# Transformer tower on one core: the second MLP product in token order, and its normalisation by statistics instructions

## What is computed

```python
x = x + attn
h2 = _ln(x, g2, beta2)                              # "norm 2"
x = x + (gelu(h2 @ w1 + b1) @ w2 + b2)              # D=256, FF=1024
...
h = h + x                                           # h: the residual of the whole tower
z = _layernorm(h)                                   # "norm 3", without gain and shift
logits = z @ gate_w.T                               # 8 experts + 1 shared
out = routed_experts(z, logits) + shared_expert(z)  # shared: silu(z @ sg) * (z @ su) @ sd
h = h + out
```

## Time and profile before

| what | value |
|---|---|
| median of 3 runs | 2754.92 us (2751.39 to 2756.34) |
| the profiled execution, its own time | 2745.01 us, of which 2743.3 us are its span |
| PE busy | 2396.6 us, 87% of the span |
| DVE busy | 1957.5 us, 71% |
| POOL busy | 1574.0 us, 57% |
| ACT busy | 1462.2 us, 53% |
| mean granted TensorE clock | 0.955 |

### The profile page before, as it was taken

One profiled execution on the slowest core, in us unless ns is written; L12 is line 12 of the kernel. 1 busy time (PEld: TensorE's weight loads), 2 busy tenths in 40 slices (PEclk: granted clock), 3 DMA queues, 4 the chain that ended last, 5 costly groups with the idle time before them and its releaser, 6 DMA issues. The chain is left out here.

```text
span 2743.3 us, 61193 instructions
## 1 busy us (share of the span) xinstructions
PE 2396.6 (87%) x22832; PEld 1736.1 (63%) x22832; DVE 1957.5 (71%) x4174; ACT 1462.2 (53%) x2731; POOL 1574.0 (57%) x1548
## 2 busy tenths in 40 slices
PE   3799999999999999999999858898988998985664
PEld 3588888878888888888887724444444444443453
DVE  2578778777877787778778735777777777775443
ACT  3566666666666666666666534443444444432232
POOL 1465656565665656565656422566556656656566
PEclk8999999999999999999999968999999999998887
DMA  4121122111221111111110020121112111100676
GB/s 146 43 67 58 40 64 61 61 43 58 62 63 40 44 37 47 36 45 39 40 44 13 10 98 24 48 85 54 48 48 84 53 43 47 38 9 16 128 136 100
DMA packets 115060, 152.21 MB, mean 55 GB/s; under 512 B 16537, under 2 KB 75917, under 8 KB 114768
## 3 DMA queue, kind: packets, MB, share of 16 engines
q1 hardware_dynamic: 88880, 124.46, 14.3%
q0 software_dynamic: 23808, 21.74, 4.4%
q10 hardware_dynamic: 2080, 2.10, 0.2%
HBM read 81.71 MB, written 90.96 MB: 63 GB/s over the span
## 5 line engine op out<-in xcount | busy, mean ns | idle before, releaser
L958 POOL TENSOR_TENSOR qkl<-fz,qkh 128x512 f16<-128x512 f32 x256 | 307.6, 1202 | 299.4 <-DVE qkh L857 299.4
L1812 POOL DMA_INDIRECT slot_dram<-xt,slot_u x256 | 257.9, 1007 | 75.8 <-issue 75.5
L529 PE MATMUL pF<-nh,qk_h 128*128 128x256 f16 x1024 | 281.2, 275 | 5.7 <-DVE nl L844 4.4
L531 PE MATMUL pF<-nl,qk_h 128*128 128x256 f16 x1024 | 280.6, 274 | 0.0
L530 PE MATMUL pF<-nh,qk_l 128*128 128x256 f16 x1024 | 280.5, 274 | 0.0
L970 POOL TENSOR_TENSOR ol<-on,oh 128x256 f16<-128x256 f32 x256 | 181.9, 711 | 147.2 <-ACT oh L794 147.1
L977 POOL TENSOR_TENSOR kvl<-kvacc,kvh 128x260 f16<-128x260 f32 x192 | 147.0, 765 | 122.3 <-ACT kvh L802 120.7
L771 ACT ACTIVATE sh<-sm 128x512 f16<-128x512 f32 x256 | 159.4, 623 | 83.6 <-DVE sm L880 83.6
L854 DVE SCALAR_TENSOR_TENSOR fz<-pF,ez 128x512 f32<-128x512 f32 x256 | 175.2, 684 | 34.1 <-ACT ez L754 32.6
L1792 POOL TENSOR_TENSOR al<-az,ah 128x512 f16<-128x512 f32 x64 | 79.2, 1238 | 206.8 <-DVE ah L1585 206.8
L529 PE MATMUL pS<-qkh 64*128 64x128 f16 x1024 | 187.7, 220 | 0.9 <-DVE sm L880 0.9
(11 more groups left out here) (315 smaller groups left out, 8667.9 us busy)
## 6 DMA issues: line engine op xcount, KB each, us to landing
xs<-in_x SPq DMA_DIRECT2D x128, 256.0 KB, 2.7
slot_dram<-blank SPq DMA_DIRECT2D x8, 1360.0 KB, 6.9
xg<-slot_dram SPq DMA_DIRECT2D x40, 272.0 KB, 3.4
h_dram<-hT SPq DMA_DIRECT2D x32, 256.0 KB, 2.3
x_dram<-x SPq DMA_DIRECT2D x32, 256.0 KB, 2.2
at_dram<-at SPq DMA_DIRECT2D x32, 256.0 KB, 2.1
x0b<-x_dram SPq DMA_DIRECT2D x16, 512.0 KB, 4.0
atb<-at_dram SPq DMA_DIRECT2D x16, 512.0 KB
```

The lines of the kernel that those rows point to most:

```text
L529: pe.matmul(out, wh, mh, start=first, stop=False, skip_group_check=True)
L531: return pe.matmul(out, wh, ml, start=False, stop=last, skip_group_check=True)
L958: nc.gpsimd.tensor_tensor(qkl[:, pair:pair + 2, cols], fz[:, n % 2, :, :], qkh[:, pair:pair + 2, cols], ALU.subtract).then_inc(fl_ready, 1)
L1812: nc.gpsimd.indirect_dma_start(io["slot_dram"], bass.IndirectOffsetOnAxis(slot_u[:, c, k:k + 1], 0), xt[:, i % 2, c, :], None, bounds_chec ...
```

## The change

The second MLP product is made with the tokens on the partitions: `gh`, `gl` are now the stationary operand and `w2_h`, `w2_l` the moving one, in 96 matmuls of 256 columns where there were 48 of 512. The residual sum `hx` comes into the same banks first, by eight float32 matmuls with a scaled identity. ACT copies the banks to `ht` (two buffers), DVE takes mean and variance of each token by `bn_stats` and `bn_aggr`, ACT makes the reciprocal root of 128x4 values, DVE makes `xn` with two per-token scalars, ACT casts it into the rows `xt` (three buffers), and POOL makes the rest. `turn_rows` now transposes those rows back, and ACT copies them to `xf`, from which `gate_up` and `logits` read. `mean3`, `var3`, `turn_sums`, `hp`, `xc3` and the squares are gone. The load of the Exp and Ln table that stood in `rstd3` stands in `logits`. `rows(i + 2)` on POOL, which makes `x1`, has a step of its own (`rows_ahead`) behind part 3 of `gate_up`.

The diff, cut to its core:

```diff
+                s["sums3"](i)
                 if after:
                     s["var2"](i + 1)
                 if after:
                     s["scale2"](i + 1)
+                s["rstd3"](i)
                 if before:
                     s["gate_up"](i - 1, after, (0,))
-                s["mean3"](i, before)
+                s["norm3"](i)
                 if after:
                     s["shift2"](i + 1)
                 if before:
-                    s["gate_up"](i - 1, after, (1, 2))
-                s["var3"](i)
+                    s["gate_up"](i - 1, after, (1,))
+                s["low3"](i, 0)
+                if before:
+                    s["gate_up"](i - 1, after, (2,))
+                s["low3"](i, 1)
                 if before:
                     s["gate_up"](i - 1, after, (3,))
-                s["rstd3"](i)
+                s["rows_ahead"](i)
                 if before:
                     s["down"](i - 1)
                 s["turn_rows"](i, before)
                 s["logits"](i)
-                s["turn_sums"](i)
...
             def w2(i, js):
-                if js[0] == 0 and not (type(i) is int and i < 2):
-                    pe.wait_ge(ob_ready, count(i, CH, -CH))
+
+                if js[0] == 0:
+                    if i == 1:
+                        pe.wait_ge(ht_ready, 2)
+                    elif i >= 2:
+                        pe.wait_ge(ob_ready, count(i, CH, -CH))
+                    pe.wait_ge(hx_ready, count(i, DT, DT))
+                    for c in range(CH):
+                        toks = slice(c * P, (c + 1) * P)
+                        for t in range(DT):
+                            at = c // 2 * D + t * P
+                            mm = pe.matmul(pY[c % 2][:, at:at + P], hx[:, t, toks], ident_w[:, :], start=c < 2 and t == 0,
+                                           stop=False, skip_group_check=True)
+                    mm.then_inc(hx_added, 1)
                 for j in js:
                     pe.wait_ge(gh_ready, count(i, FT, j + 1))
                     pe.wait_ge(gl_odd if j % 2 else gl_even, count(i, FT // 2, j // 2 + 1))
-                    for m in range(DT):
-                        cols = slice(m * P, (m + 1) * P)
-                        mm = three(pY[m][:, :], w2_h[:, j, cols], w2_l[:, j, cols], gh[:, j, :], gl[:, j, :],
-                                   j == 0, j == FT - 1)
+                    for c in range(CH):
+                        toks = slice(c * P, (c + 1) * P)
+                        mm = three(pY[c % 2][:, c // 2 * D:(c // 2 + 1) * D], gh[:, j, toks], gl[:, j, toks],
+                                   w2_h[:, j, :], w2_l[:, j, :], False, j == FT - 1)
                 if js[-1] == FT - 1:
                     mm.then_inc(w2_done, 1)

-            def mean3(i, before):
-                pe.wait_ge(hp_ready, count(i, DT, DT))
-                if before:
-                    pe.wait_ge(lg_ready, count(i, 1, 0))
-                for t in range(DT):
-                    mm = pe.matmul(pL[:, :], ones[:, :], hp[:, t, :], start=(t == 0), stop=(t == DT - 1))
-                mm.then_inc(mean3_done, 1)
...
             def logits(i):
-                pe.wait_ge(rs3_step, count(i, 2, 1))
-                pe.wait_ge(xnh_ready, count(i, DT, DT))
-                pe.wait_ge(xnl_ready, count(i, DT, DT))
+                pe.wait_ge(xf_ready, count(i, 2, 2))
+                if i > 0:
+                    pe.wait_ge(lg_ready, count(i, 1, 0))
...
             def turn_rows(i, before):
-                pe.wait_ge(xnh_ready, count(i, DT, DT))
-                pe.wait_ge(xnl_ready, count(i, DT, DT))
                 for half in range(2):
+                    pe.wait_ge(xnh_ready, count(i, 2, half + 1))
+                    pe.wait_ge(xnl_ready, count(i, 2, half + 1))
                     if half == 0:
                         if before:
                             pe.wait_ge(az_ready, count(i, ST, 0))
...
                             pe.wait_ge(xc2_ready, count(i + 1, DT, DT))
                             pe.wait_ge(rs2_step, count(i + 1, 2, 1))
                     bank16 = pA[half][:, :].bitcast(F16)
-                    for c in range(2):
-                        toks = slice((2 * half + c) * P, (2 * half + c + 1) * P)
-                        for part, src in enumerate((xnh, xnl)):
-                            for t in range(DT):
-                                w = (c * 2 + part) * DT + t
-                                mm = pe.transpose(bank16[:, w * P:(w + 1) * P], src[:, t, toks], ident16[:, :])
+                    for part in range(2):
+                        for t in range(DT):
+                            for c in range(2):
+                                w = (part * DT + t) * 2 + c
+                                words = slice((part * DT + t) * P // 2, (part * DT + t + 1) * P // 2)
+                                mm = pe.transpose(bank16[:, w * P:(w + 1) * P],
+                                                  xt[:, i % XT, 2 * half + c, words].bitcast(F16), ident16[:, :])
                     mm.then_inc(xt_done, 1)
-
...
+            def sums3(i):
+                act.wait_ge(w2_done, count(i, 1, 1))
+                if i >= 2:
+                    act.wait_ge(ob_ready, count(i, CH, -CH))
+                for b in range(2):
+                    nc.scalar.activation(ht[:, i % 2, b:CH:2, :], pY[b][:, :].rearrange("p (c n) -> p c n", c=2), ACT.Copy,
+                                         scale=1 / W2_SCALE).then_inc(ht_ready, 1)
+
+            def rstd3(i):
+                act.wait_ge(mv3_ready, count(i, CH, CH))
+                nc.scalar.activation(ln3[:, :], mv3[:, :, 1], ACT.Ln, bias=EPS).then_inc(rs3_step, 1)
+                act.wait_ge(rs3_step, count(i, 2, 1))
+                if i > 0:
+                    act.wait_ge(xn_ready, count(i, CH, 0))
+                nc.scalar.activation(rs3[:, :], ln3[:, :], ACT.Exp, scale=-0.5).then_inc(rs3_step, 1)
+
+            def norm3(i):
+                if i >= XT:
+                    act.wait_ge(rows_sent, count(i - XT + 1, 16 * CH * TOP, 0))
+                    act.wait_ge(xt_done, count(i - XT, 2, 2))
+                for half in range(2):
+                    act.wait_ge(xn_ready, count(i, CH, 2 * half + 2))
+                    nc.scalar.activation(xt[:, i % XT, 2 * half:2 * half + 2, 0:D // 2].bitcast(F16),
+                                         xn[:, 2 * half:2 * half + 2, :], ACT.Copy).then_inc(xnh_ready, 1)
...
+                exp_ln_tables(nc, act)
...
             def turn_rows(i, before):
                 for half in range(2):
                     act.wait_ge(xt_done, count(i, 2, half + 1))
-                    if i >= 2:
-                        act.wait_ge(rows_sent, count(i - 1, 16 * CH * TOP, 0))
-                    nc.scalar.activation(xt[:, i % 2, 2 * half:2 * half + 2, 0:ROW_ID].bitcast(F16),
-                                         pA[half][:, :].bitcast(F16).rearrange("p (c n) -> p c n", c=2),
-                                         ACT.Copy).then_inc(xt_ready, 1)
-
...
+                    if i > 0:
+                        act.wait_ge(gu_done, count(i, 2 * ST, 0))
+                        act.wait_ge(lg_done, count(i, 1, 0))
+                    nc.scalar.activation(xf[:, :, :, half * 2 * P:(half + 1) * 2 * P].rearrange("p a t n -> p (a t) n"),
+                                         pA[half][:, :].bitcast(F16).rearrange("p (w n) -> p w n", n=2 * P),
+                                         ACT.Copy).then_inc(xf_ready, 1)
...
+            def sums3(i):
+                if i > 0:
+                    ve.wait_ge(rs3_step, count(i, 2, 0))
+                    ve.wait_ge(xn_ready, count(i, CH, 0))
+                for b in range(2):
+                    ve.wait_ge(ht_ready, count(i, 2, b + 1))
+                    for c in (b, b + 2):
+                        nc.vector.bn_stats(st3[:, c, :], ht[:, i % 2, c, :]).then_inc(st3_ready, 1)
+                    for n, c in enumerate((b, b + 2)):
+                        ve.wait_ge(st3_ready, count(i, CH, 2 * b + n + 1))
+                        nc.vector.bn_aggr(mv3[:, c, :], st3[:, c, :]).then_inc(mv3_ready, 1)
+
+            def norm3(i):
+                ve.wait_ge(rs3_step, count(i, 2, 2))
+                ve.wait_ge(mv3_ready, count(i, CH, CH))
+                if i > 0:
+                    ve.wait_ge(xnh_ready, count(i, 2, 0))
+                    ve.wait_ge(xnl_ready, count(i, 2, 0))
+                for c in range(CH):
+                    nc.vector.tensor_scalar(xn[:, c, :], ht[:, i % 2, c, :], mv3[:, c, 0:1], rs3[:, c:c + 1],
+                                            ALU.subtract, ALU.mult).then_inc(xn_ready, 1)
...
+            def low3(i, half):
+                gp.wait_ge(xnh_ready, count(i, 2, half + 1))
+                if half == 0 and i >= XT:
+                    gp.wait_ge(rows_sent, count(i - XT + 1, 16 * CH * TOP, 0))
+                    gp.wait_ge(xt_done, count(i - XT, 2, 2))
```

(23 more changed lines are left out.)

137 lines of the change are left out of this document (39 added, 98 removed).

## The result

The kernel after took 2831.06 us, median of four runs (2825.76 to 2835.57), against 2755.63 us for the kernel before on the same chip (four runs, 2751.39 to 2760.83): 1.0263 times as long, 95% interval 1.0239 to 1.0287. The forecast was 2760, its range 2740 to 2778.

The account below looks back on a forecast made before the run. It took chains on DVE, ACT and POOL, not PE's work, as the bound: +0.87 us a body, +12 over fourteen, less 5 in body 0 and 2 at the end, +5 on the median 2754.92: 2760, range 2740 to 2778.

Parts of the forecast that it names:

- ACT copies lg at D+3.5: After D, the end of down: ACT copies the logits 3.5 us later, taking 0.21, then loads the Exp table.
- DVE is free at M+4.06: After M, the first counting matmul: DVE finishes its routing links 4.06 us later, and the statistics follow.
- The ends: Outside the repeated bodies: body 0 about 5 us earlier, and 2 us saved on POOL's sends at the end.
- First gelu: Behind down, after the logits copy and table loads: first gelu at D+6.52, where it was D+7.66.
- hx, 2.0 us: Ahead of the second MLP product: 16 float32 passes add 2.0 us on PE; rival 4.8 us, chance 0.04.
- DVE's chain to the mask, 20.47 us: From the cast of the first gelu to the mask written: DVE without a gap, 20.47 us as before.
- D to M: From the end of down to the first counting matmul: 27.86 us, 1.14 less, with PE waiting 1.3 for the mask.
- Statistics, 2.2 us: After M+4.06 on DVE: four bn_stats and four bn_aggr replace hp and take 2.2 us, ending at M+6.3.
- The first xn held, az 1 late, TensorE idle for 6 us before part 3: M to D: POOL's hx holds the first xn 1.2 us; part 3 starts at M+18.3, PE idle 6 us.
- Half clock behind that wait, 1.7 us lost: Part 3 of gate_up after PE's idle wait: half clock makes it 2.6 + 1.7 us.
- lasts through part 3: Rival: half clock through part 3 and most of down, 3 us lost, 2778; chance 0.20 shared with dear statistics.
- M to D: From the first counting matmul to the next end of down: 27.9 us, growing by 2.0.

Follow-up runs that it names:

- late chips: Measurements where TensorE's signals were seen late, a state not a piece of hardware; kernel after against before there: ratio 1.0263.
- twelfth run: The kernel before, unchanged, run again for its trace where signals were late: 2756.51 us.
- prompt chip: Measurements where TensorE's signals were not seen late; the unchanged kernel after took 2748.28 us there, ratio 1.001 to before.
- sixteenth run: Kernel after with GpSimd's two hx instructions moved ahead of al 0, signals prompt: 2758.95 us, ratio 1.0046 to before.

## Why the prediction was wrong, and where it was right

**The step that failed** is one that the prediction never wrote down: that a signal is seen when the work is done. It put the time between the end of TensorE's work and its reader at next to nothing. "ACT copies lg at D+3.5" was D+5.6 in the body shown, and "DVE is free at M+4.06" was M+8.04. Both hang on instructions that wait for TensorE while GpSimd sends rows, and that waited 2.3 and 4.1 us on average where the sum had 0.2. The trace of before had no hint of it: its own lag was 0.18 us in every body, and that trace, at 2745.01 us, was a prompt one; the runs beside it, 2751 to 2756, look like those of the late chips (2757 and 2758), and not like those of the prompt ones (2744 to 2747). The prediction saw those 0.36% and carried them over as an offset. By the twelfth run, which has the late signals at 2756.51 us, they were most likely the first sign of them, small because the kernel before covers them; but the runs beside the first trace were not traced. The change removed the cover. It took TensorE's rest ahead of the counts (2.58 us in the earlier trace rows, mostly under 0.5 after) and put the logits, which had been read when ACT came free anyway, on the chain in the middle of the sends.

**On a prompt chip the steps can be held against the trace**, and the sum is +3.2 us (2748.23 against 2745.01, profiled executions) for a forecast of +5. That the two are so close is partly luck: a body costs 0.3 us more than before and not 0.9, and a loss behind body 0 that the sum hadn't takes its place ("The ends", below).

- *First gelu.* lg at D+3.43, gelu at D+6.49 (predicted 3.5 and 6.52). Right where signals are prompt.
- *hx, 2.0 us.* Sixteen passes in 1.95 us. Right; at 4.8 us D to M would have shown it.
- *DVE's chain to the mask, 20.47 us.* It took 19.16 (1953.67 to 1972.83). Its holds by GpSimd (four instructions much longer than their like) sum to 3.0 us instead of 4.4, since the sends and gl stand otherwise against it. So the mask is 1.3 us earlier and the wait of 1.3 us before the counting is gone: TensorE reaches it at the same moment. D to M is 27.0 on average for 27.86.
- *Statistics, 2.2 us.* 1.84 us (1976.94 to 1978.78). In the line groups of the same trace:

```profile
L1575 DVE TENSOR_SCALAR xn<-ht,mv,rs 128x256 f32<-128x256 f32 x64 | 34.6, 599 | 0.5
L1563 DVE BATCH_NORM_STATS2 st<-ht 128x6 f32<-128x256 f32 x64 | 23.6, 410 | 10.1 <-ACT ht L1455 9.6
L1566 DVE BATCH_NORM_AGGREGATE mv<-st 128x2 f32<-128x6 f32 x64 | 9.6, 173 | 0.0
```

- *The first xn held, az 1 late, TensorE idle for 6 us before part 3.* 2.27 us for xn, and 5.90 us idle at M+17.8 (predicted M+18.3). Right, and the sixteenth run shows the hold by removing it.
- *Half clock behind that wait, 1.7 us lost.* Its record of 0.61 us opens a stretch at half clock that lasts until 1995.75 (granted clock 0.50), the whole of part 3: 5.1 us for 2.6 of work, 2.5 lost where the sum had 1.7. Part of the rival "lasts through part 3" was true. M to D is 28.0 on average (27.9).
- *The ends.* The first gelu of body 1 came 4.6 us earlier (5 forecast), and from the first gelu of body 15 to the last send the kernel after took 1.5 us less (2). But by the first gelu of body 2 only 0.7 of the 4.6 was left: 3.9 us lost where I had 0.9. From there to body 15 it lost another 3.9, where I had 11. Why body 1 is so dear I haven't followed up.

The rival on the slower side was half clock; the real one was missing from the list. The sum of a body was within 0.8 us where signals are prompt (55.75 for 55.02), 5.3 off where they aren't (61.08). No row of that trace could have given late signals a chance; two traces of before from different hours could have.

**What stays open.** Why signals are late in one measurement and not in another, with the same kernel and the same sends. What the runs show is when: only on a late chip, and only beside back-to-back sends (not in body 0, nor in the breaks of the train, nor at a signal whose sends were moved away). They are mostly later the less TensorE rests ahead (2.9 us from the start of its last record, in the twelfth run: 1.3 us; 0.1 to 0.6 us, in the kernel after: mostly 4.3). That is no rule: with one-pass matmuls for hx 1.9 us of rest went with 4.2, and body 15 has 10 us of rest and lags of 0.2 to 2.1. Nor does it strike every engine's signals: DVE's, that the mask is written, comes in the middle of the train, and in the first late trace TensorE starts 0.06 us behind it in most bodies. The recorder itself may have a part: the late traces lack 2,600 to 2,900 of some 21,900 semaphore updates, and in the first of them 2,235 of the 2,776 that the prompt trace has more are landings of these very sends. The Trainium skill ("NOTIFIC — the notification-queue block", Overflow: three behaviours, one of which stalls the engine) says that the notification block's inner pipeline pushes back on its producers rather than lose a record. No run here shows that this happens; the updates that are missing are lost somewhere all the same; and as each run here comes with recorded spans and clocks, none shows the kernel without the recorder.

## What to carry to other kernels

Before you explain a difference of some per cent, run the unchanged kernel again beside the experiment, and compare lags from an engine's last record to its reader: two sets of well-meant experiments here measured the chip. Keep back-to-back indirect sends away from a signal of TensorE's on which the chain hangs, if there is a free place for them: moved away from the counts they cost nothing on a prompt chip, and on a late one the ratio was 1.005, after 1.026 in another measurement without the move; moved away from the logits they ran into GpSimd's own work and cost 28 us. And when GpSimd's arithmetic holds a small DVE instruction, look at what it will hold in its new place before you move it.

## What was not expected of the hardware

- In 9 of 20 traces, of kernels as different as before and after, the signal of a finished TensorE group was seen up to 5.4 us late beside indirect sends, and signals of three groups came within 0.13 us. In the other 11 the median signal of TensorE's came 0.014 us behind the end of its record, and none in this stage over 0.03 us.
- A DVE copy of 128x4 took 3.16 us beside two GpSimd additions of 128x512, for 0.17 us alone, and a DVE tensor_tensor of 128x32 took 3.07 for 0.19.
- A kernel can hide such a lag: the kernel before, with 1.3 us of it, lost nothing in twelve of its bodies, as DVE had a wait of 1.21 us to give, and the change took that cover away.
